# Two layers of cross attention on one core: where key sums, square transposes and a layer norm stand in the order

## The reference

```python
# first layer: one head of 512
q = x @ w_q.T;  k = ctx @ w_k.T;  v = ctx @ w_v.T
x = x + alpha * (softmax(q @ k.T / sqrt(512)) @ v) @ w_o.T
# then two layers of 16 heads of 128, each on the same context
def cross_attention(h, ctx):                       # per layer
    qh, kh, vh = h @ wq + bq, ctx @ wk + bk, ctx @ wv + bv
    kh, vh = concat(kh, bias_k), concat(vh, bias_v)   # one more token
    return softmax(qh @ kh.T / sqrt(128)) @ vh @ wo + bo
x = x + cross_attention(layer_norm(x), ctx)        # twice
x = x + gelu(layer_norm(x) @ w_fc1 + b_fc1) @ w_fc2 + b_fc2
```

## Time and profile before

| | |
|---|---|
| time, median of 3 runs (lowest, highest) | 1748.85 us (1745.42, 1750.02) |
| the profiled execution: its own time, its span | 1745.42 us, 1743.6 us |
| PE busy | 1721.1 us, 99% of the span |
| VectorE, ScalarE, POOL busy | 68%, 43%, 50% |
| chain that ended last | PE 92%, DVE 5%, ACT 1%, DMA 1% |
| HBM | 89 GB/s over the span |

### The profile page before, as it was taken

One profiled execution on the slowest core, in us unless ns is written; L12 is line 12 of the kernel. 1 busy time (PEld: TensorE's weight loads), 2 busy tenths in 40 slices (PEclk: granted clock), 3 DMA queues, 4 the chain that ended last, 5 costly groups with the idle time before them and its releaser, 6 DMA issues.

```text
span 1743.6 us, 30234 instructions
## 1 busy us (share of the span) xinstructions
PE 1721.1 (99%) x10854; PEld 1674.9 (96%) x10854; DVE 1190.7 (68%) x2718; ACT 752.0 (43%) x1624; POOL 872.1 (50%) x727
## 2 busy tenths in 40 slices
PE   8999999999998999999999999999999999999999
PEld 4899999999998999999999999999999999999999
DVE  3667676666877766667876666668766666677675
ACT  3634334334553333335453344345533333454654
POOL 2684252455583453534873523555834535336754
PEclk9999999999999999999999999999999999999999
DMA  7732332223452322324342323234423223204432
GB/s 278 253 117 79 89 89 51 71 84 97 138 157 64 81 83 70 90 50 142 115 126 74 86 49 76 83 106 131 145 57 83 63 75 86 79 19 142 132 128 80
DMA packets 162784, 175.09 MB, mean 100 GB/s; under 512 B 99660, under 2 KB 115276, under 8 KB 162636
## 3 DMA queue, kind: packets, MB, share of 16 engines
q1 hardware_dynamic: 159388, 168.86, 33.2%
q10 hardware_dynamic: 3248, 4.30, 0.7%
HBM read 150.67 MB, written 5.14 MB: 89 GB/s over the span
## 4 chain that ended last, share of the span: by engine, by line
PE 92%; DVE 5%; ACT 1%; DMA 1%; issue 1%; SPq 1%; ACTq 0%; DVEq 0%
PE psum L819 29%; PE psum L820 29%; PE psum L821 29%; PE psum L1157 2%; PE psum L853 2%; DVE key_stage_late L1710 1%; DMA key_stage_late<-head_w_dram 1%; DVE prob L1989 1%; DVE pT L1684 1%; DVE centred L1890 0%; SPq L563 0%; PE psum L832 0%; DVE a_lo L1684 0%; PE psum L828 0%; ACT prob L1520 0%
## 5 line engine op out<-in xcount | busy, mean ns | idle before, releaser
L653 POOL TENSOR_TENSOR wbuf_hi<-stage,zero_col 128x512 fp32r<-128x512 f32 x256 | 273.1, 1067 | 667.5 <-PE psum L821 503.4
L708 POOL TENSOR_TENSOR wbuf_lo<-stage,wbuf_hi 128x512 fp32r<-128x512 f32 x256 | 337.5, 1318 | 20.1
L819 PE MATMUL psum<-pT,ctx_rows_hi 128*128 128x250 f32 (+1 forms) x1152 | 330.4, 287 | 6.7 <-DVE pT L1684 6.5
L820 PE MATMUL psum<-pT,ctx_rows_hi 128*128 128x250 f32 (+1 forms) x1152 | 330.2, 287 | 0.0
L821 PE MATMUL psum<-pT,ctx_rows_lo 128*128 128x250 f32 (+1 forms) x1152 | 329.6, 286 | 0.0
L819 PE MATMUL psum<-ctxT_hi,a_hi 128*125 128x362 f32 (+1 forms) x832 | 277.1, 333 | 0.5
L821 PE MATMUL psum<-ctxT_hi,a_lo 128*125 128x362 f32 (+1 forms) x832 | 273.0, 328 | 0.0
L820 PE MATMUL psum<-ctxT_lo,a_hi 128*125 128x362 f32 (+1 forms) x832 | 273.0, 328 | 0.0
L819 PE MATMUL psum<-a_hi,wbuf_hi 128*128 128x400 f32 x720 | 253.3, 352 | 0.9 <-DVE xT L1905 0.9
L820 PE MATMUL psum<-a_lo,wbuf_hi 128*128 128x400 f32 x720 | 247.6, 344 | 0.0
L821 PE MATMUL psum<-a_hi,wbuf_lo 128*128 128x400 f32 x720 | 247.5, 344 | 0.0
(11 more groups left out here) (220 smaller groups left out, 3384.8 us busy)
## 6 DMA issues: line engine op xcount, KB each, us to landing
stage<-head_w_dram SPq DMA_DIRECT2D x256, 256.0 KB, 2.9
mlp_stage<-mlp_w_dram SPq DMA_DIRECT2D x32, 512.0 KB, 3.3
ctx_rows_in<-ctx_dram SPq DMA_DIRECT2D x20, 768.0 KB, 4.5
ctxT_in<-ctxT_dram SPq DMA_DIRECT2D x20, 724.0 KB, 4.8
p_b<-p_scratch SPq DMA_DIRECT2D x64, 200.0 KB, 3.5
sorted<-prob SPq DMA_DIRECT2D x256, 48.0 KB, 2.0
key_stage<-head_w_dram SPq DMA_DIRECT2D x22, 256.0 KB, 5.1
pT<-prob SPq DMA_DIRECT2D x96, 48.0 KB, 2.0
```

The source lines that it names most:

```text
L653: return nc.gpsimd.tensor_tensor(out, in_, zero_col[0:in_.shape[0], :].broadcast_to(tuple(in_.shape)), ALU.add)
L708: nc.gpsimd.tensor_tensor(lo, held, hi.bitcast(F32), ALU.subtract).then_inc(stage_free, 1)
L819: pe.matmul(out, a_h, x_hi, start=start, stop=False)
L820: pe.matmul(out, a_h, x_lo, start=False, stop=False)
```

## The change

Seven things, in the order of the file. (1) The ten late key sums are made in phase 0 only, two in each of five steps (places "a" and "b" of the step), not five in phase 0 and five in phase 1; SP loads them at other places. (2) `in_squares` holds for x = 0 only: the blocks (1,1,1), (1,2,1), (2,2,1), (3,1,1), (3,2,1) and (4,2,1) of every phase are turned by PE. (3) SP issues all sorts of a place ahead of the loads of `p_b`, whatever block these need. (4) PE's products for the hidden mean and variance stand behind the scores of block 1. (5) ScalarE's four squares stand together behind the probabilities of (5,1,0). (6) On VectorE, the additions of piece `o` come behind normalise; centring comes behind normalise of block 1; the inversions stand between the `lo` parts of the attended context. (7) In the single head two `lo` parts of the context's columns come earlier.

```diff
-LATE_KEYS_IN = 2
-LATE_KEYS_AT = [(0, 1), (0, 2), (0, 3), (1, 2), (1, 3)]
-FIRST_LATE_KEY_BEHIND = 9
-LATE_KEYS_BEHIND_SORTED = [(0, 2, 0), (0, 3, 0), (1, 0, 0), (1, 3, 0)]
+LATE_KEYS_AT = {(0, 1): "ab", (0, 2): "ab", (0, 3): "ab", (1, 2): "ab", (1, 3): "ab"}
+LATE_KEYS_BEHIND = {8: 1, 18: 1, 20: 1, 21: 1}
+LATE_KEYS_BEHIND_SORTED = {(0, 1, 0): 2, (0, 2, 0): 2, (0, 3, 0): 2}
...
-    return 0 < k + (x == 0) and k < len(UNITS) - 1 and not (k in LATE and b < 2) and not (x == 1 and b in (0, NB - 1))
+    return k < len(UNITS) - 1 and x == 0 and not (k in LATE and b < 2)
-HELD = 2
+HELD = 1
...
# SP
-                            while reads and T_AT[LAST_BLOCK_OF[reads[0]]] < T_AT[at]:
-                                load_first_probs(ph, reads.pop(0))
                             sort_squares(ph, *at)
-                            if ph < LATE_KEYS_IN and at in LATE_KEYS_BEHIND_SORTED:
+                            for _ in range(LATE_KEYS_BEHIND_SORTED.get(at, 0) if ph == 0 else 0):
                                 load_late_key_weights(next(keys))
-                    for h in reads:
-                        load_first_probs(ph, h)
+                    for h in VALUES:
+                        if P0_READ_AT[h] == i and UNIT_OF[h] < LAST_UNIT:
+                            load_first_probs(ph, h)
...
# PE
                         scores(k, b, 0)
-                        if (k, b) == MEAN_IN:
-                            hidden_mean()
                         if before is not None:
                             turn_probs(*last)
                         run_pieces((k, b, "a"))
+                        scores(k, b, 1)
                         if (k, b) == VARIANCE_IN:
                             hidden_variance()
-                        scores(k, b, 1)
+                        if (k, b) == MEAN_IN:
+                            hidden_mean()
...
# VectorE
-                        run_pieces((k, b, "a"), 0, added_first)
                         normalise(k, b, 0)
-                        run_pieces((k, b, "a"), added_first)
+                        run_pieces((k, b, "a"))
...
+                        if ph == 0 and "a" in LATE_KEYS_AT.get((k, b), ""):
+                            late_key_sums(next(keys))
                         maxima(k, b, 1)
+                        normalise(k, b, 1)
                         if (k, b) == MEAN_IN:
                             hidden_centre(ph)
                         if (k, b) == VARIANCE_IN:
-                            hidden_invert(ph, 0, DC - 1)
-                        normalise(k, b, 1)
-                        if before is not None:
+                            for part in range(DC - 1):
+                                attended_lo(*before, part, part + 1)
+                                hidden_invert(ph, part, part + 1)
+                            attended_lo(*before, DC - 1, DC)
+                        elif before is not None:
                             attended_lo(*before)
```

More of the change, by code:

```diff
@@ L90 @@
 KEYS = 7
-LATE_KEYS_IN = 2
-LATE_KEYS_AT = [(0, 1), (0, 2), (0, 3), (1, 2), (1, 3)]
-FIRST_LATE_KEY_BEHIND = 9
-LATE_KEYS_BEHIND_SORTED = [(0, 2, 0), (0, 3, 0), (1, 0, 0), (1, 3, 0)]
-KEYS_BEFORE = LAYERS * H - LATE_KEYS_IN * len(LATE_KEYS_AT)
+LATE_KEYS_AT = {(0, 1): "ab", (0, 2): "ab", (0, 3): "ab", (1, 2): "ab", (1, 3): "ab"}
+LATE_KEYS_BEHIND = {8: 1, 18: 1, 20: 1, 21: 1}
+LATE_KEYS_BEHIND_SORTED = {(0, 1, 0): 2, (0, 2, 0): 2, (0, 3, 0): 2}
+KEYS_BEFORE = LAYERS * H - len("".join(LATE_KEYS_AT.values()))
 PHASES = [(half, l) for l in range(LAYERS) for half in range(HALVES)]
@@ L427, in in_columns @@
             return ap.rearrange("p t (a j) -> p t a j", j=SQUARE)
-        held = [sorted0[:, :, :]] + [pT[:, 0:GROUPS, WIDE - RUN:WIDE].bitcast(F32)]
+        held = [sorted0[:, :, :]]
         def held_chunks(j):
@@ L558, in sort_squares @@
                     sp.wait_ge(p0_sent[x], 32 * n)
-                if x == 1:
-                    wait(sp, u_mm, ph * U_LAYER)
                 for a in range(GROUPS):
@@ L589, in _ @@
                 for i in range(early + 2 * (ph > 0), W_AT["v", H - 1]):
-                    reads = [h for h in VALUES if P0_READ_AT[h] == i and UNIT_OF[h] < LAST_UNIT]
                     for at in IN_SQUARES:
                         if SORTED_AT[at] == i:
-                            while reads and T_AT[LAST_BLOCK_OF[reads[0]]] < T_AT[at]:
-                                load_first_probs(ph, reads.pop(0))
                             sort_squares(ph, *at)
-                            if ph < LATE_KEYS_IN and at in LATE_KEYS_BEHIND_SORTED:
+                            for _ in range(LATE_KEYS_BEHIND_SORTED.get(at, 0) if ph == 0 else 0):
                                 load_late_key_weights(next(keys))
-                    for h in reads:
-                        load_first_probs(ph, h)
+                    for h in VALUES:
+                        if P0_READ_AT[h] == i and UNIT_OF[h] < LAST_UNIT:
+                            load_first_probs(ph, h)
                     load_weights(ph, i)
-                    if ph < LATE_KEYS_IN and i == FIRST_LATE_KEY_BEHIND:
-                        load_late_key_weights(next(keys))
+                    if ph == 0:
+                        for _ in range(LATE_KEYS_BEHIND.get(i, 0)):
+                            load_late_key_weights(next(keys))
                     if i == X_BEHIND:
@@ L1431, in norm_hi, with hidden_squares @@
                                              bias=norm_p[:, PARAMETERS[j], c, OFFSET_COL:OFFSET_COL + 1]).then_inc(n_hi, 1)
-            def hidden_square(ph, c):
-                act.wait_ge(hn_cen, ph * DC + c + 1)
-                nc.scalar.activation(x_held[:, c, :], centred[:, c, :], ACT.Square).then_inc(hn_sq, 1)
+            def hidden_squares(ph):
+                for c in range(DC):
+                    act.wait_ge(hn_cen, ph * DC + c + 1)
+                    nc.scalar.activation(x_held[:, c, :], centred[:, c, :], ACT.Square).then_inc(hn_sq, 1)
             def hidden_roots(ph):
@@ L1482, in queries_hi @@
                 def queries_hi(h):
-                    if ph < LATE_KEYS_IN and h == ASIDE[0]:
-                        act.wait_ge(kw_sum, KEYS_BEFORE + (ph + 1) * len(LATE_KEYS_AT))
+                    if ph == 0 and h == ASIDE[0]:
+                        act.wait_ge(kw_sum, LAYERS * H)
                     nc.scalar.activation(made_queries(h)[0], made("q", h), ACT.Identity, bias=bias_of(BQ, h))\
@@ L1605, in layer @@
                         probs_hi(k, b, 0)
+                        if (k, b) == MEAN_IN:
+                            hidden_squares(ph)
                         run_pieces((k, b, "b"))
@@ L1801, in single_head @@
                 turned_lo(0)
+                ctx_columns_lo(1, 0)
                 queries1_lo(1)
@@ L1805, in single_head @@
                 probs0_lo(2)
-                ctx_columns_lo(1, 0)
+                ctx_columns_lo(1, 1)
                 queries1_lo(2)
@@ L1964, in add_output, with run_pieces @@
                         add(columns(xT[:, m, :]), made("o", h, m), columns(xT[:, m, :]), l, m, h == 0).then_inc(y_done, 1)
-                def run_pieces(place, start=0, stop=None):
-                    for kind, h in pieces(place)[start:stop]:
+                def run_pieces(place):
+                    for kind, h in pieces(place):
                         {"q": queries_lo, "k": through_keys_lo, "v": values_lo, "o": add_output}[kind](h)
@@ L2088, in layer @@
                             hidden_scale(ph, 0, 1)
-                    if ph < LATE_KEYS_IN and (k, b) in LATE_KEYS_AT:
+                    if ph == 0 and "b" in LATE_KEYS_AT.get((k, b), ""):
                         late_key_sums(next(keys))
-                    if ph == LATE_KEYS_IN - 1 and (k, b) == (3, 2):
+                    if ph == 0 and (k, b) == (3, 2):
                         key_parts(1)
```

4 lines of the change are left out of this document (removed).

## The result

The changed kernel takes 1770.01 us (median of 4 runs, 1768.51 to 1772.52) against 1747.13 us before (4 runs, 1744.16 to 1750.02): ratio 1.0133, 95% interval 1.0109 to 1.0155. It is 22.9 us slower. The forecast had slower, by 10.7 (1759.5); its whole range ended at 1771, its own, without the rivals, at 1766. The profiled execution took 1768.73 us, its span is 1766.9 us.

What follows compares the result with a forecast made beforehand. PE's own stream was taken as the bound; 7.7 - 6.2 + 3.8 + 1.2 + 4.2 = +10.7 us on the profiled 1745.4 gave 1756.1, or a median of 1759.5 us. Range 1749 to 1771 with rivals, 1754 to 1766 its own.

Steps and rivals of the forecast that it cites:

- turns: Six x = 1 blocks a phase go back to PE, 24 turns at 0.32 us each: +7.7 us.
- late sums: Ten key sums in phase 0: 9.7 us given back, phase 0 loses 3.5: -6.2 us.
- additions: Steps (1,3) and (3,3) of four phases: PE waits 0.47 us for output added behind normalise: +3.8 us.
- `p_b`: Step (1,1): VectorE stands 6 us for probability rows; PE's attend waits some 0.3 a phase for q5's bank: +1.2 us.
- hidden norm: Unit 5: moved squares and reciprocals make PE wait 1.05 us in each of four phases: +4.2 us.
- single head: Two low parts of the context moved ahead, where VectorE waited for ScalarE: 0, within 0.5 us either way.
- the slowest landing: Step (1,1), upper end for the late loads of `p_b`: 1.4 us a phase, 5.6 in all.
- the three waits: Unit 5: PE waits 0.35 us each for the variance, at turn (5,2,1) and for normalise (5,2,2).
- POOL in the way: Unit 5, upper end of the hidden norm's cost: 2 us a phase, 8 in all.
- VectorE's slack absorbs everything: Between attend's end and the next bank need, three wait terms (9.2 us) vanish: median 1750.3, not slower; 15%.
- Late sums choke phase 0: Loads of 7.0 us or POOL in most sums cost phase 0 10 or more us: +17.2, 1766; 14%.
- transposes at full price: On PE, 72 transposes in a row at 0.27 us, 19.4 instead of 7.7: +22.4, 1771; 4%.

Runs made afterwards that it cites:

- half of edit 7: The kernel before with only the second low part of the context's columns moved up behind the first, which stays in place: 1749.01 us, ratio 0.9995.

## Why the direction was right and the size half of it

The sum, term by term, as the runs have it: turns 7.9, late sums -4.7 (from the steps of the changed kernel), additions 5.9, `p_b` 6.6, hidden norm 7.0, single head 2.6, together 25.3 against 22.9 measured (turns and hidden norm from the runs alone, additions and `p_b` from the changed kernel without them, the head from its later end of 2.58). It need not close better: the terms have intervals of 2 to 5 us each way, and what late sums, additions and `p_b` cost together in phase 0 stands in more than one of them. The forecast had 7.7, -6.2, 3.8, 1.2, 4.2 and 0. What was mis-sized is above all `p_b`, then the hidden norm and the head.

- *Turns*: right, 0.34 each instead of 0.32. The 275 ns of the Trainium skill (TensorE: Matmul & The Clock Gate, Part 4: PE-mode transpose), near the 0.27 that the rival took, is a duration and not a price in a row: three cost 0.34.
- *Late sums*: right in mechanism and nearly in size. The sixth sum was forecast to end near 182.1 and PE to start at 183.3 to 183.7; with the 2.58 us by which the head is later, the trace has 184.7 and 185.85. Phase 0 lost 5.2 instead of 3.5, as unit 1 cost more than the 1.0 set for its four sums, 2.3, of which 1.1 come with edit 1 alone, and step (3,3) 0.6 more at `key_parts`. That comes only with the additions: without them the step is 0.36 longer, one turn.
- *Additions*: right, 0.56 a place in unit 3 (forecast 0.47), and more in the two places named above. Alone the same edit costs 10.7. The turns take 0.25 a place off (0.80 to 0.55 in unit 3), since PE comes 0.34 later to the bank; most of the rest is phase 1, where the places cost 3.4 and 3.6 alone and 1.0 and 0.55 in the changed kernel, as edit 1 has taken late sums and `key_parts` out of it.
- *`p_b`*: this step failed. VectorE was forecast to stand 6 us; it stood 6.94 in phase 2: the first load, issued at 945.28, is used 4.3 us later, where the forecast set 3.5 from the sorts' end. Worse, the row of work worked forward from there looked for the bank of q5 at attend alone. Two earlier needs were left out: the bank of v1, where PE waits in the kernel with edit 3 alone, and the turn of block (1,1,1), which edit 2 adds and which needs the normalised block. That is 1.4 us a phase in phases 2 and 3, the upper end that the forecast had for the slowest landing, and 6.6 in all where the sum had 1.2.
- *Hidden norm*: the three waits were forecast at 0.35 each. The two by the inversions came as said in phases 2 and 3 (0.5 + 0.17) and less behind the wait for `square_sum` in phases 0 and 1 (0.09 + 0.17); measured alone they are 2.8 in four phases. The wait for `square_sum` is 0.76 and 0.77 in phases 0 and 1: POOL's first add starts 2.28 us behind the turn of (5,1,0) where the forecast's row had 1.94, and its last piece took 1.25 instead of 1.05. The forecast's own row is too late by a slip: 435.2 + 0.96 + 3.3 + 0.93 + 1.05 is 441.44, not 441.65. In phases 2 and 3 it does not show, because PE is held up before, at turn (5,1,2). There the reason is one the forecast had only as an upper end (POOL in the way): VectorE and POOL of the changed kernel, phase 2:

```profile
1192.51 1.28 DVE L1986 TENSOR_SCALAR prob<-prob,stats 100x384 f32<-100x384 f32 x1
```

```profile
1190.29 3.28 POOL L736 TENSOR_TENSOR x_held<-x_held 128x400 f32<-128x400 f32 x3 [5.78 <-ACT x_held L1432]
```

  With the squares together POOL's three adds stand together too and cover the normalising, 0.42 us in the earlier trace rows, which ends at 1193.79, 0.2 behind POOL. Mean product 0.22 a phase: costed at nothing, but it stood ahead of turn (5,0,2), which waits now, 0.48 to 0.80 us in the four phases. POOL is in this wait too (the normalise ahead of the row at 807.91 took 1.02), and it varies from execution to execution: the run of edit 7 alone has 0.86, 0.72 and 0.91 there in three phases, without any edit of the hidden norm. So up to some tenths a phase of the 7.0 may be no cost of these edits.
- *Single head*: costed at 0 within 0.5, as it falls where VectorE waits. It also falls beside POOL's 3.5 us instruction; the price is 2.3 to 2.6, far beyond the 0.5 set for it.

Of the rivals, *VectorE's slack absorbs everything* fell as the runs with one edit show; the slack is real but smaller than each of these waits. *Late sums choke phase 0* fell. The measured time lies at that of *transposes at full price* by coincidence; the turns alone refute it. It is also luck that the time lies in the whole range: it is above the forecast's own range (1754 to 1766) and below 1771 only because this rival's price had set that end.

## What to carry to other kernels

When an engine is going to stand for some microseconds, list everything that the bottleneck asks of it afterwards, in order, including what another edit of the same change adds; the first need decides, not the one that is best known. An order by hand that looks free (VectorE waits there anyway) has to be laid beside POOL's row as well, because one long instruction of POOL there is a stop for VectorE's work on SBUF. Edits that load one engine don't add up: the additions cost 10.7 us alone and 5.9 in company, and `p_b` 13.6 and 6.6, so a single-edit run says which edits are bad but not what each gives back.

## What the runs showed of the hardware that was not expected

- Three kinds of VectorE instructions that read SBUF alone and started while a POOL instruction ran ended 0.15 to 1.5 us behind POOL, in less than their usual time: a `lo` part of 1.73 became 4.65 us, a scaling of 0.42 became 1.28, a sum's 0.28 became 1.37. It goes the other way too: in the kernel with half of edit 7 a POOL product of 1.3 us, started behind VectorE's `lo` part, took 2.72. The Trainium skill (SBUF — State Buffer, section SBUF: two separate sides) has it as an exclusive lock of the ports that the two share, held for a whole instruction by whichever starts first, where VectorE has two inputs in SBUF or runs in a mode that uses both its port pairs; the traces agree. The forecast used this for the late sums, had it as an upper end in the hidden norm, and overlooked it in the head.
- The granted clock can fall after short idle times of PE, and does so in some executions and not in others. Of the 38 waits of 1.5 to 2.7 us behind the start in the fourteen profiles, 14 were followed within 1.6 us by a stretch at 1.2 GHz, one of them a wait of 1.73, and 24 were not, one of them of 2.71. After the wait of 1.9 us near 66 us the changed kernel's profile stays at 1.00, while that of edit 7 alone, with the same wait, has 0.91 over 66 to 84 us and starts its first phase 1.5 us later. It also fell with no wait ahead: five of the profiles here have 0.76 over 108 to 122 us, where the kernel before has 1.00, though PE had last waited (0.5 us) near 96 us and had run matmuls since; their first phase starts 2.3 to 2.8 us later. Turns alone, and before:

```profile
108.00:122.00 14.00, 13.83 (x71) 0.76 0.29 83
108.00:122.00 14.00, 12.99 (x88) 1.00 0.32 93
```

  So over 2 us of the difference of two profiles can be the clock's, and the runs' medians are the measure.
